# Twenty-nine short identity products in place of twelve longer ones, with the four lists of steps placed anew

## The reference, cut to what matters

```python
sa, ca, ga, sb, cb, gb = (silu(c) @ wmod) split in six       # ga, gb kept away from zero
h = layernorm(x) * (1 + ca) + sa
x = x + ga * attn(h)      # linear attention with two decays, 16 heads of 8
h = layernorm(x) * (1 + cb) + sb
x = x + gb * ffn(h)       # gate, up, down; inputs and weights rounded to fp4 in blocks of 16

# attn: q, k, v, three gates of h; M_fast, M_slow = sums over all tokens of k * v with weights
# that need a suffix sum of logarithms over the tokens; o = alpha * q M_fast + (1 - alpha) * q M_slow
```

## Time and profile before

| | |
|---|---|
| median of 3 runs | 199.48 us (198.5 to 200.17) |
| the profiled execution | 199.69 us |
| its span, first to last instruction | 197.7 us |
| busy: TensorE, weight loads | 184.5 us, 144.9 us |
| busy: VectorE, GpSimd, ScalarE | 161.1 us, 160.9 us, 133.8 us |

### The profile page before, as it was taken

The page is one execution under the profiler, slowest core; times in us unless marked ns, Lnnn a source line. Parts: engine busy times, 40 slices in busy tenths (PEclk is TensorE's granted clock), DMA queues, the critical chain, the costliest instruction groups (busy, mean ns, idle before and its releaser), DMA issues.

```text
span 197.7 us, 3626 instructions
## 1 busy us (share of the span) xinstructions
PE 184.5 (93%) x1022; PEld 144.9 (73%) x1022; DVE 161.1 (81%) x408; ACT 133.8 (68%) x319; POOL 160.9 (81%) x205
## 2 busy tenths in 40 slices
...
## 3 DMA queue, kind: packets, MB, share of 16 engines
q1 hardware_dynamic: 11320, 6.36, 11.4%
q10 hardware_dynamic: 312, 0.13, 0.2%
...
## 4 chain that ended last, share of the span: by engine, by line
PE 45%; POOL 24%; issue 15%; DVE 10%; ACT 3%; DMA 1%; POOLq 0%; DVEq 0%; ACTq 0%
PE pa L1085 9%; POOL q_r L498 6%; POOL q_o L510 6%; PE pa L1189 4%; PE pv L1021 4%; PE pg L1119 4%; PE pv L1191 4%; POOL kw L454 3%; DVE q_x L958 3%; PE pv L1153 3%; PE pa L1213 2%; POOL rstdb L477 2%; POOL xn L411 2%; PE pa L1200 2%; DVE q_r L961 2%
## 5 line engine op out<-in xcount | busy, mean ns | idle before, releaser
L498 POOL TENSOR_TENSOR q_r<-q_x,q_rs 128x960 f32<-128x960 f32 (+2 forms) x18 | 29.5, 1640 | 10.8 <-DVE q_rs L950 10.3
L510 POOL TENSOR_TENSOR q_o<-q_r,q_sp 128x960 f32<-128x960 f32 (+2 forms) x18 | 29.5, 1641 | 7.4 <-DVE q_r L961 7.2
L1189 PE MATMUL pa<-guT,hqT 128*128 128x352 f32 x64 | 25.2, 475 | 2.5 <-ACT hqT L708 2.4
L1213 PE MATMUL pa<-wdg,fqT 128*128 128x128 f32 x192 | 27.3, 278 | 0.1
L717 ACT ACTIVATE sgl<-pa 128x352 f32<-128x352 f32 x32 | 14.6, 462 | 15.0 <-PE pa L1189 12.0
L1213 PEld LDWEIGHTS pa<-wdg,fqT 128*128 128x128 f32 x192 | 24.0, 192 | 1.0 <-ACT fqT L725 0.4
L1191 PE MATMUL pv<-guT,hqT 128*128 128x352 f32 x64 | 24.3, 461 | 0.3 <-DVE x_all L913 0.3
L1085 PE MATMUL pa<-wcat,hT 128*128 128x368 f32 x64 | 23.7, 504 | 0.0
L702 ACT ACTIVATE q_A<-q_r 128x960 f32<-128x960 bf16 (+2 forms) x18 | 16.0, 888 | 11.4 <-DVE q_r L961 6.2
L958 DVE SCALAR_TENSOR_TENSOR q_x<-q_A,q_r 128x960 f32<-128x960 f32 (+2 forms) x18 | 18.5, 1029 | 4.6 <-ACT q_A L702 4.6
L454 POOL TENSOR_TENSOR kw<-kg,cw 128x256 f32<-128x256 f32 x32 | 19.6, 636 | 1.8 <-DVE cw L864 1.8
...
## 6 DMA issues: line engine op xcount, KB each, us to landing
...
```

The costliest lines, as they stand in the source:

```text
L498: g.tensor_tensor(blocks(q_r[:, s % 2, c]), blocks(q_x[:, s % 2, c]), spread(q_rs[:, s % 2, n]), ALU.mult)\
L510: g.tensor_tensor(blocks(q_o[:, s % 2, c]), blocks(q_r[:, s % 2, c]), spread(q_sp[:, s % 2, n]), ALU.mult)\
L1189: te.matmul(bank_a(("G%d" % k, i))[:, 0:I], lhs, guT[:, 0, :], start=True, stop=True)\
L1213: last = te.matmul(t[:, k * D:(k + 1) * D], fqT[:, (2 * i + k) % 4, ch * P:(ch + 1) * P], wdg[:, b % 2, ch, :], start=False, stop=(ch == 2))
```

## The change

FI has 128 columns in place of 256, and there are 29 of it in place of 12, so 3712 columns in place of 3072. The first two stand at the head of TensorE's list, ahead of CT. Fourteen stand ahead of PP:0 in place of four, and fifteen behind it in place of eight. All four lists are written out again; the set of the other steps is the same on every engine.

```diff
     "tensor": """
-        CT:0 FI:0 RP:0 FI:1 WK:0 FI:2 CM:0 WQ:0 PX:0 FI:3 KW:0 PX:1 PX:2 PP:0 PP:1 PX:3 PP:2 PP:3 PX:4 FI:4
+        FI:0 FI:1 CT:0 FI:2 FI:3 FI:4 FI:5 FI:6 FI:7 WK:0 FI:8 FI:9 RP:0 FI:10 FI:11 CM:0 WQ:0 PX:0 KW:0 PX:1
+        FI:12 FI:13 PP:0 PX:2 PP:1 PX:3 PP:2 PP:3 FI:14 PX:4 FI:15 PX:5 FI:16 FI:17 PX:6 PP:4 MR:0 FI:18 FI:19
...
             def FI(_):
                 pe.wait_ge(S["ident"], 1)
-                te.matmul(pv[NBANK_V - 1][:, 0:2 * P], ident[:, :], ident[:, None, :].broadcast_to([P, 2, P]),
-                          start=True, stop=True)
+                te.matmul(pv[NBANK_V - 1][:, 0:P], ident[:, :], ident[:, :], start=True, stop=True)
```

More of the change, by code:

```diff
@@ L67 @@
+        QR:14 QO:13 L1:11 O3:12 QO:14 O3:13 QR:15 GH:2 L1:12 QO:15 L1:13 QR:16 O3:14 O3:15 QR:17 QO:16 L1:14
+        QO:17 GH:3 L1:15 QR:18 QR:19 QO:18 QO:19 QR:20 QR:21 QO:20 QO:21""",
     "scalar": """
-        CT:0 WK:0 CM:0 WQ:0 PX:0 KW:0 PX:1 PX:2 PP:0 PP:1 PX:3 PP:2 PP:3 PX:4 PX:5 GT:0 PX:6 PP:4 GA:0 PP:5
-        W1:0 PP:6 PX:7 GD:0 PX:8 GS:0 PP:7 GE:0 GT:1 PX:9 BV:0 PX:10 GA:1 PP:8 NC:0 PP:9 PX:11 PP:10 GG:0 GD:1
-        PP:11 GS:1 O2:0 PX:12 GE:1 O2:1 GT:2 PP:12 PX:13 O2:2 GA:2 L1:0 NC:1 PX:14 PP:13 GG:1 L1:1 QA:4 PP:14
@@ L71 @@
[L71 to L75, removed]
@@ L87 @@
-    "tensor": """
-        CT:0 FI:0 RP:0 FI:1 WK:0 FI:2 CM:0 WQ:0 PX:0 FI:3 KW:0 PX:1 PX:2 PP:0 PP:1 PX:3 PP:2 PP:3 PX:4 FI:4
[L89 to L98, removed]
+        CT:0 WK:0 CM:0 WQ:0 PX:0 KW:0 PX:1 PP:0 PX:2 PP:1 PX:3 PP:2 PP:3 PX:4 PX:5 GT:0 PX:6 PP:4 GA:0 PP:5
@@ new lines @@
+        PP:6 W1:0 GD:0 PX:7 PX:8 GS:0 PP:7 GE:0 GT:1 PP:8 PX:9 GA:1 BV:0 NC:0 PX:10 PP:9 PX:11 PP:10 GG:0
+        PX:12 GD:1 GS:1 O2:0 PP:11 GE:1 O2:1 PX:13 O2:2 GT:2 GA:2 PP:12 L1:0 NC:1 PX:14 PP:13 PX:15 L1:1 PP:14
+        GG:1 QA:4 GD:2 O2:3 N4:0 L1:2 QA:5 O2:4 PP:15 W3:0 F1:0 GS:2 O2:5 GT:3 O2:6 GA:3 QA:6 L1:3 NC:2 N4:1
+        L1:4 GE:2 F1:1 N4:2 GG:2 F1:2 L1:5 QA:7 F3:0 GD:3 QA:8 O2:7 O2:8 F4:0 N4:3 O2:9 F1:3 L1:6 N4:4 GS:3
+        F1:4 F3:1 QA:9 F4:1 QA:10 F3:2 O2:10 GE:3 N4:5 L1:7 NC:3 F1:5 N4:6 L1:8 F1:6 GG:3 F3:3 QA:11 L1:9
@@ new lines @@
+        O2:11 F4:2 QA:12 F3:4 F4:3 N4:7 L1:10 F1:7 N4:8 F3:5 F1:8 O2:12 QA:13 F4:4 L1:11 F3:6 QA:14 O2:13 F4:5
+        N4:9 F1:9 O2:14 F3:7 N4:10 QA:15 L1:12 L1:13 O2:15 F1:10 F4:6 N4:11 F3:8 F1:11 QA:16 F4:7 F3:9 L1:14
+        F4:8 QA:17 F4:9 N4:12 L1:15 F1:12 N4:13 F1:13 F3:10 QA:18 F4:10 F3:11 QA:19 F4:11 N4:14 F3:12 F1:14
+        N4:15 F1:15 QA:20 F4:12 F3:13 QA:21 F4:13 F3:14 F4:14 F3:15 F4:15""",
+    "vector": """
+        P0:0 XN:0 MV:0 XN:1 CB:0 XN:2 P0:1 XN:3 PP:0 PP:1 P0:2 GA:0 PP:2 PP:3 W1:0 PP:4 PP:5 PP:6 GK:0 MR:0
+        GE:0 GF:0 GA:1 PP:7 P0:3 PP:8 GY:0 GK:1 GG:0 W2:0 O1:0 PP:9 GE:1 O1:1 GF:1 O1:2 GA:2 PP:10 PP:11 O3:0
+        O3:1 O3:2 L1:0 L1:1 GY:1 GK:2 GG:1 PP:12 Q:4 PP:13 PP:14 QT:4 O1:3 GE:2 O1:4 Q:5 L1:2 O1:5 O3:3 GF:2
+        GA:3 PP:15 O1:6 QT:5 O3:4 F1:0 Q:6 O3:5 O1:7 L1:3 L1:4 GK:3 QT:6 O3:6 GG:2 GY:2 F1:1 L1:5 Q:7 F1:2 Q:8
+        O1:8 QT:7 GE:3 O1:9 O1:10 QT:8 L1:6 O3:7 GF:3 F1:3 Q:9 F1:4 Q:10 O1:11 QT:9 O3:8 QT:10 L1:7 O3:9 O3:10
+        L1:8 F1:5 GG:3 Q:11 GY:3 F1:6 Q:12 L1:9 QT:11 O1:12 O1:13 QT:12 L1:10 O3:11 F1:7 Q:13 L1:11 F1:8 Q:14
+        QT:13 O3:12 O1:14 QT:14 O3:13 F1:9 Q:15 L1:12 L1:13 O1:15 O3:14 QT:15 F1:10 Q:16 O3:15 F1:11 L1:14
+        Q:17 QT:16 QT:17 L1:15 F1:12 Q:18 F1:13 Q:19 QT:18 QT:19 F1:14 Q:20 F1:15 Q:21 QT:20 QT:21""",
```

31 lines of the change are left out of this document (15 added, 16 removed).

## The result

The changed kernel takes 203.24 us (median of 4 runs, 202.91 to 203.42) against 198.99 us for the kernel before on the same chip (4 runs, 198.19 to 200.17): the ratio is 1.0227, 95% interval 1.0184 to 1.0271. It is slower by over 1%; the interval doesn't say whether it is slower by 2%. The forecast was 197.6 and the range ended at 200.6. The profiled execution took 203.21 us, with a span of 201.5 us.

A forecast was written before the change was run, and what follows sets the result against it. It saw no engine filling the span and time to be had in the first 20 us, where TensorE starts at half clock. Gains of 1.7 to 2.2 us, taken as 1.9, off 199.48 gave 197.6; range 195.6 to 200.6.

The forecast's parts named there:

- Identity, CT, FI, rise of the clock at 6.7, PP:0 at 9.5: Start of TensorE: dense work from 1.55 us lifts the clock at 6.7; PP:0 starts 0.7 to 0.9 us earlier.
- ScalarE 2.2 ahead behind PP:3: First four PP at full clock rate: PP:3 ends on ScalarE at 15.9 instead of 18.10, 2.2 us ahead.
- zb at 16.4: VectorE after the statistics of batch 2: zb comes at 16.4 us, 1.7 earlier.
- GpSimd at GC:0: GpSimd reaches GC:0 1.8 us ahead, since lf, which it waits for, comes 1.8 earlier.
- XN:7 in the hole: GpSimd ahead of P0:2: XN:7 fills its 2.09 us idle time and is out of the way later.
- wm 3 us earlier, W2 meets XN:12, O1:0 at 41.7: Around the first wm: it comes 3 us earlier, XN:12 is slowed to 3.25, O1:0 starts at 41.7, leaving 1.9.
- What the clock's rise is worth: TensorE's earlier full rate at the start: the clock's own part is 2.2 us on ScalarE, 1.1% of 199.5.
- the sum: Whole kernel: the gain adds up to 1.7 to 2.2 us, taken as 1.9.
- L1:0 at 55.2, QR:4 at 57.8, net 1.7: GpSimd up to the first rounding: L1:0 at 55.2 against 56.55, QR:4 2.4 us earlier, net gain 1.7.
- From there the lists are all but the same ... ends earlier by it: After the first rounding: every engine starts earlier by the same amount, so the pipeline ends earlier by it.
- the clock falls back: Rival: half rate returns for PP:4 to PP:7, plus 4.9 less 1.9, giving 202.5 us; chance 0.09.
- Absorbed, because collisions fall differently: Rival: up to 60 us one engine, VectorE, gets no earlier; gain 0 to 1, time 198.5 to 199.5; chance 0.13.

The follow-up runs named there:

- before_l18: Kernel before, with VectorE's L1:8 moved behind O3:10 as in the change: 200.45 us, ratio 1.008 to the kernel before.
- tail_new: Kernel before with its 12 products up to about 80 us, the change's lists from there on: 200.95 us, ratio 1.0133.
- after_l18: Changed kernel with VectorE's L1:8 back ahead of O3:9 and O3:10: 199.56 us, ratio 1.006 to the kernel before.

## Why the prediction was wrong, step by step

- **Identity, CT, FI, rise of the clock at 6.7, PP:0 at 9.5:** right (1.57, 6.57, 9.61). ScalarE 2.2 ahead behind PP:3: 1.7 in the trace. zb at 16.4: 16.41. GpSimd at GC:0: 22.04 against 24.16, so 2.1 ahead where 1.8 was forecast; XN:7 in the hole. Right.
- **wm 3 us earlier, W2 meets XN:12, O1:0 at 41.7:** right (GG at 38.59 against 41.82, six XN in 4.86, PX:12 0.60 late, O1:0 at 41.50).
- **What the clock's rise is worth:** mis-sized, through a run that was taken for the rule. The profiled execution of before had its rise at 13.52; before_l18 and tail_new, with the same products at the same places, had it near 12.2 and 9.7, and their first q_am at 57.67 and 56.20 against 58.17. An early rise was no gain over such runs. The products alone, in the lists of before, are 1.7 below the profiled execution of before (197.95 against 199.69), but 0.8 below its median (0.5% by the ratio); the sum had 1.9. The forecast also started from 199.48, a median of three runs, where the larger groups have 198.1 to 198.9.
- **L1:0 at 55.2, QR:4 at 57.8, net 1.7:** the first step that failed. I summed GpSimd's list and did not follow VectorE's O3:0, which the new list puts behind PP:10 and PP:11. L1:0's first pass came at 57.42, QR:4 at 59.99. 1.49 of the 2.2 us by which L1:0 missed are GpSimd's wait for O3:0, which the sum had at nothing. In the end O3:0's place cost about 1.1, and the whole head 1.8.
- **"From there the lists are all but the same ... ends earlier by it":** the step that failed by most. One step, L1:8 on VectorE, behind O3:10 rather than ahead of O3:9, cost 3.7 where the sum had nothing: 2.16 by two blocked instructions and 1.6 by the clock that fell behind them. after_l18 and before_l18 show it from both sides.
- **The rivals:** "the clock falls back" had the sign and nearly the time (202.5), but not the cause: it was to come at 15 to 30 us. It came at 126, behind a stall that another engine had made. "Absorbed, because collisions fall differently" had the mechanism and priced it at a lost gain only. I had given the meeting of W2 and XN a price from its row and never asked what the next one would cost where a step moves by 0.05 us.
- **Two slips that change nothing:** fifteen FI of 0.22 are 3.3 us, not 3.2, and half of 0.45 with 0.20 is 0.43, not 0.44.

The sum that holds: 198.6 less 0.8 for the products, plus 1.8 for the head, plus 2.2 for the meeting, plus 1.6 for the clock, is 203.4 against 203.24. It was made after the runs and is no test of its own.
